# First half's mixes: who reads the transposes' bank, and who hands it back

## The reference

```
xn = layernorm(x)
xs = shift of xn by one token (zero first)
xm = xn * time_mix + xs * (1 - time_mix)          # the "mix"
k = exp(min(xm @ Wk.T, 60)); v = xm @ Wv.T; r = xm @ Wr.T
wkv, sum_k = decaying sums over earlier tokens of k*v and of k, per channel
attn = (sigmoid(r) * wkv / sum_k) @ Wo.T
z   = layernorm(xn) * ln_gamma + ln_beta
gamma = max |z| over the WHOLE input               # needs every token before any use
ffn = clip(z * 128 / gamma) @ ternary(weight) * (gamma * beta / 128)
out = x + attn + ffn
```

## Time and profile before

| what | value |
| --- | --- |
| median of three runs | 912.33 us |
| profiled execution | 912.93 us, span 911.1 us |
| TensorE busy | 878.0 us, 96% |
| VectorE busy | 761.6 us, 84% |
| ScalarE busy | 509.1 us, 56% |
| GpSimd busy | 188.5 us, 21% |
| share of TensorE in the chain that ended last | 71% (VectorE 17%, ScalarE 4%) |
| line 590 (removed operation) | 32 times, 21.7 us, mean 679 ns |
| line 861 (VectorE's mix before) | 32 times, 22.2 us, mean 696 ns |

### The profile page before, as it was taken

One profiled execution on the slowest core, in us unless ns is written; L12 is line 12 of the kernel. 1 busy time (PEld: TensorE's weight loads), 2 busy tenths in 40 slices (PEclk: granted clock), 3 DMA queues, 4 the chain that ended last, 5 costly groups with the idle time before them and its releaser, 6 DMA issues.

```text
span 911.1 us, 12736 instructions
## 1 busy us (share of the span) xinstructions
PE 878.0 (96%) x3984; PEld 713.5 (78%) x3984; DVE 761.6 (84%) x1282; ACT 509.1 (56%) x830; POOL 188.5 (21%) x242
## 2 busy tenths in 40 slices
PE   2989999999999999999999999999999999999998
PEld 2768777787878777787888888888888888888886
DVE  5998988889798988889897887878878878789684
ACT  3674756757575756747555464653635545455441
POOL 5442334134243323231010010100201002011000
PEclk9999999999999999999999999999999999999999
DMA  8221405142321405144543444243432543334311
GB/s 277 105 81 73 159 26 186 32 150 70 138 92 69 162 7 179 56 150 109 190 133 122 139 151 153 68 159 138 147 107 79 196 138 98 109 128 139 93 47 46
DMA packets 59841, 107.13 MB, mean 118 GB/s; under 512 B 7712, under 2 KB 7712, under 8 KB 59808
## 3 DMA queue, kind: packets, MB, share of 16 engines
q1 hardware_dynamic: 59808, 106.73, 34.8%
HBM read 64.76 MB, written 41.96 MB: 117 GB/s over the span
## 4 chain that ended last, share of the span: by engine, by line
PE 71%; DVE 17%; issue 5%; ACT 4%; DMA 1%; SPq 0%; DVEq 0%; ACTq 0%
PE kvr L492 13%; PE kvr L494 13%; PE kvr L493 13%; PE out_banks L528 6%; PE out_banks L530 6%; PE out_banks L507 6%; PE out_banks L510 6%; PE out_banks L509 6%; DVE scans L942 4%; DVE bn_stats L805 2%; PE transposed L450 2%; DVE rwkv_lo L962 1%; DVE k_and_kv L932 1%; DVE absmax L868 1%; DVE k_and_kv L958 1%
## 5 line engine op out<-in xcount | busy, mean ns | idle before, releaser
L1195 POOL TENSOR_TENSOR evacuated<-normed,mix_over_ffn_row 128x512 f32<-128x512 f32 x28 | 36.3, 1298 | 353.2 <-DVE ffn_lo L885 353.2
L492 PE MATMUL kvr<-xm_hi,wk_hi 128*128 128x512 f32 x256 | 103.8, 405 | 4.0 <-DVE xm_lo L885 4.0
L492 PE MATMUL kvr<-xm_hi,wv_hi 128*128 128x512 f32 x256 | 102.8, 402 | 1.4 <-DVE k_and_kv L932 0.9
L492 PE MATMUL kvr<-xm_hi,wr_hi 128*128 128x512 f32 x256 | 103.4, 404 | 0.0
L507 PE MATMUL out_banks<-wo_hi,rwkv_hi 128*128 128x512 f32 x256 | 101.9, 398 | 0.5 <-DVE rwkv_lo L962 0.5
L510 PE MATMUL out_banks<-wo_hi,rwkv_lo 128*128 128x512 f32 x256 | 101.2, 395 | 0.0
L509 PE MATMUL out_banks<-wo_lo,rwkv_hi 128*128 128x512 f32 x256 | 101.2, 395 | 0.0
L494 PE MATMUL kvr<-xm_hi,wk_lo 128*128 128x512 f32 x256 | 100.8, 394 | 0.0
L494 PE MATMUL kvr<-xm_hi,wr_lo 128*128 128x512 f32 x256 | 100.5, 393 | 0.0
L493 PE MATMUL kvr<-xm_lo,wk_hi 128*128 128x512 f32 x256 | 100.4, 392 | 0.0
L493 PE MATMUL kvr<-xm_lo,wr_hi 128*128 128x512 f32 x256 | 100.1, 391 | 0.0
(11 more groups left out here) (125 smaller groups left out, 1910.1 us busy)
## 6 DMA issues: line engine op xcount, KB each, us to landing
other<-ffn_input SPq DMA_DIRECT2D x64, 256.0 KB, 5.4
x<-in_x SPq DMA_DIRECT2D x15, 1024.0 KB, 5.8
other<-in_x SPq DMA_DIRECT2D x8, 1024.0 KB, 5.6
ffn_input<-evacuated SPq DMA_DIRECT2D x32, 256.0 KB, 4.6
ffn_input<-parked SPq DMA_DIRECT2D x32, 256.0 KB, 2.1
attn_scratch<-x SPq DMA_DIRECT2D x8, 1024.0 KB, 4.4
parked<-attn_scratch SPq DMA_DIRECT2D x8, 1024.0 KB, 7.2
out<-parked SPq DMA_DIRECT2D x8, 1024.0 KB, 5.2
```

What stands on the lines that cost most here:

```text
L492: nc.tensor.matmul(KVR[:, m, :], hi, XH[t][:, ch, :], start=(ch == 0), stop=False)
```

## The change

In the first half VectorE takes the token's own part from the transposes' bank and multiplies it by `time_mix` in the same operation that adds the shifted part. ScalarE makes the shifted part alone. As VectorE is now the last reader of the bank, TensorE's slots wait for `dve_x` besides `act_u`.

```diff
             def slot(b, ph, n):
                 kind, ch = slot_of(ph, n)
+
+                pe.wait_ge(dve_x, splits_before(b, ph, n))
                 pe.wait_ge(act_u, slots_before(b, ph, n))
...
                 elif mix:
-                    if ph != "P":
-                        nc.scalar.activation(U[:, r, :], bank, ACT.Copy, scale=tmx[:, ch:ch + 1])
                     nc.scalar.activation(WS[:, n % 2, :], bank, ACT.Copy,
                                          scale=tmx1[:, ch:ch + 1]).then_inc(act_u, 1)
...
                 dve.wait_ge(act_u, m + 1)
-                if ph == "P":
-
-                    bank, scale = first_banks[n], tmx[:, ch:ch + 1]
-                    V.tensor_copy(last_x[:, ch:ch + 1], WS[:, n % 2, TILE - 1:TILE])
-                    V.tensor_scalar(U[:, r, 0:1], bank[:, 0:1], scale, None, ALU.mult)
+                if kind.startswith("mix") and ph != "B":
+
+                    bank, scale = first_banks[n] if ph == "P" else TB[:, :], tmx[:, ch:ch + 1]
+                    if kind.endswith("0"):
+                        V.tensor_copy(last_x[:, ch:ch + 1], WS[:, n % 2, TILE - 1:TILE])
+                        V.tensor_scalar(U[:, r, 0:1], bank[:, 0:1], scale, None, ALU.mult)
+                    else:
+                        V.scalar_tensor_tensor(U[:, r, 0:1], bank[:, 0:1], scale, last_x[:, ch:ch + 1],
+                                               ALU.mult, ALU.add)
                     V.scalar_tensor_tensor(U[:, r, 1:TILE], bank[:, 1:TILE], scale, WS[:, n % 2, 0:TILE - 1],
                                            ALU.mult, ALU.add).then_inc(dve_x, 1)
...
-                elif kind.startswith("mix"):
-
-                    if kind.endswith("0"):
-                        V.tensor_copy(last_x[:, ch:ch + 1], WS[:, w, TILE - 1:TILE])
-                    else:
-                        V.tensor_tensor(U[:, r, 0:1], U[:, r, 0:1], last_x[:, ch:ch + 1], ALU.add)
-                    V.tensor_tensor(U[:, r, 1:TILE], U[:, r, 1:TILE], WS[:, w, 0:TILE - 1],
-                                    ALU.add).then_inc(dve_x, 1)
```

## The result

The changed kernel took 955.42 us (median of 4 runs, 953.61 to 957.15) against 912.45 us for the one before. The ratio is 1.0465, 95% interval 1.0452 to 1.0477: slower by 43 us. The forecast was 951.3, range 939 to 957.

What follows compares the result with a forecast made beforehand. TensorE, busy 96%, was taken to bound the kernel. Waits of 32.3 less 4.5 us given back, plus 11.2 us of lower clock, made 39.0 us on 912.93 profiled; 951.3 us as median, range 939 to 957.

Steps and rivals of the forecast that it cites:

- What bounds the kernel: Whole kernel: TensorE, busy 96% of the span; time is lost or won where it stands still.
- First hand-over: Slots 8 to 9 and 20 to 21, eight groups: TensorE waits for VectorE's late mix, 32.3 us in all.
- Second and third hand-over: Slots 9 to 10 to 11 and 21 to 22 to 23: no further waits; 4.5 us given back at the third.
- the 4.5 us given back: Third hand-overs, slots 11 and 23: old waits vanish as ScalarE has one bank read and TensorE comes later.
- not slower: Rival: first slot's mix done before TensorE wants the bank; 908 us; chance 0.05 together with "no change".
- TensorE's clock: Behind the long first hand-over pauses: granted clock falls at seven of eight, 1.6 us each, 11.2 us in all.
- the one case before: Batch 0, before the transposes at 54.40: a 2.69 us pause, then a clock fall taken to cost 1.6 us.
- upper bound of 19 us: Clock term's upper limit: all eight pauses bring the fall, with a stretch half as long again at the lower level.
- The sum: Whole kernel: 27.8 us of net waits plus 11.2 us of clock, 39.0 us on the profiled 912.93.
- the mechanism that came true: First half: TensorE's standstill plus the fall of its clock, range 947 to 955 us, chance 0.70.
- every hand-over waits: Rival: third and sometimes second hand-overs fail by 0.5 us; 955 us, up to 959; chance 0.12.
- The second half: Second half of the kernel: no instruction changes, so it should last the same.

Runs made afterwards that it cites:

- the wait alone: The kernel before, with only TensorE's slots also waiting for VectorE's `dve_x`; ScalarE still makes both parts: 957.77 us, ratio 1.049.
- one mix moved: The changed kernel, with VectorE's mix of slots 8 and 20 moved ahead of the two scans of the recurrence: 920.50 us, ratio 1.0086.
- the relief of ScalarE without the long pauses: The changed kernel without the second semaphore; in the first half VectorE multiplies its SBUF buffer's contents instead of reading the bank: 911.13 us, ratio 0.9978.
- the busy pauses: The changed kernel, with 12 extra matmuls of unused result before the waiting transposes of slots 9 and 21: 939.14 us, ratio 1.0289.
- two mixes early: The changed kernel, with VectorE's mixes of slots 8 and 20 before the recurrence's scans and of 9 and 21 behind them: 915.21 us, ratio 1.0025.
- the same order with the old mix: The kernel before, with mixes of slots 8, 9, 10, 20, 21, 22 early and ScalarE reading 10 and 22 before the logarithm: 912.30 us, ratio 0.9994.

## Why the prediction was right, and the term that was too small

- *What bounds the kernel.* TensorE, and its pauses: right. The loss lies in the distances between its transposes, at the first and second hand-overs.
- *First hand-over.* 32.3 us forecast, 32.6 measured, eight waits of 2.3 to 4.5 us. The lag could be read from the trace before because VectorE's backlog there waits for nobody. The run with the wait alone brings the pauses back with the old mix, and the run with one mix moved takes them away. VectorE's pair takes 175.90 - 175.03 = 0.87 us in `mix_own1`, 0.88 forecast; from PSUM the wide operation takes 0.74 us, as the rows before had it. The 62 more cycles of the Trainium skill (VectorE: DVE Perf Modes, the section on the TRN2 errata) show in none of these rows.
- *Second and third hand-over.* No further waits: right, and the 4.5 us given back came as 4.4. But the relief of ScalarE without the long pauses gives only 1.9 us. In that run the third hand-overs got 2.7 us shorter and not 4.5: those of `mix_next0` still took 3.6 to 3.7 us instead of 3.2. And 1.6 us came back as waits at the output product. In the changed kernel, where TensorE's pauses let VectorE catch up, all of them took 3.2. The rival "not slower" named 908 us for a kernel without long pauses; the run that comes nearest to it took 911.1. Its gain of 4.5 us was too high by 2.6.
- *TensorE's clock.* The mechanism was right, the term "7 x 1.6 = 11.2 us" mis-sized: it measured 17.1 us in the trace, and 16.3 us by the busy pauses. Two things were off. All eight pauses brought the fall, that of 2.29 us too, which the prediction had left out for being shorter than the one in the trace before (2.69). And the one case before was at the cheap end: the eight cost 1.46 to 2.85 us, 2.1 on average, since the lower level lasted from about 3 to 6 us. The upper bound of 19 us given for this term held. That one case was also weaker ground than it looked: the same pause, 2.69 to 2.74 us in all ten profiles, brought no fall in two of them (two mixes early, and the same order with the old mix). The seven pauses of 3.7 us and more all brought it, here and in the run with the wait alone.
- *The sum.* It has 39.0 us of loss, the profile 43.2. The clock is 5.9 us more than forecast, and the first and third hand-overs are 0.4 more (32.6 - 4.4 against 27.8). The distances elsewhere, which the sum put at nothing, are 2.1 us less. So two errors in part cancelled, and the total came nearer than its largest term. The result also lies just past the 947 to 955 us given to the mechanism that came true, where "every hand-over waits" was priced; that rival did not happen, as the second hand-overs waited for nobody and the third ones took 3.2 us.
- *The second half.* Unchanged: right, 474.3 against 474.1 us.

## What to carry to other kernels

When a buffer of which there is only one gets a new last reader, look up in the trace when that reader comes to the operation, not how long it takes: here 0.87 us of work handed the bank back 4 us late, because it stood behind a backlog that had cost nothing so far. Each of the eight pauses of the matmul engine, 2.3 to 4.5 us long, cost another 1.5 to 2.9 us of slow matmuls behind it, so count a long pause with more than its own length. Where the new reader must stay, move its operation in its queue and follow what the move delays, on both engines: the first move here brought back 35 us, the next ones ran into the logarithm behind the recurrence and then into the last low part.

## What the runs showed of the hardware

- All 14 pauses of TensorE of 3.67 to 4.46 us (changed kernel and the wait alone) were followed by a stretch at 1.2 GHz. Of the 12 of 2.19 to 2.74 us in the ten profiles, 10 were, and two, of 2.71 and 2.70 us, were not. The two shortest of these, 2.19 and 2.29 us, came only 7 us behind another pause, so they may not stand for their length alone. Behind pauses of 1.10 to 1.80 us in front of slots 9, 10, 21 and 22 the next slot came in 3.2 to 3.3 us, with no sign of a fall.
- The length of one pause doesn't settle it. In the start of the kernel before, the level fell with shorter pauses, where TensorE did only three matmuls between them, 18.16 and 20.42 us into the profile:

```profile
18.16 0.47 PE L492 MATMUL kvr<-xm_hi,wk_hi 128*128 128x512 f32 x1 [1.71 <-DVE xm_lo L885]
20.42 0.79 PE L492 MATMUL kvr<-xm_hi,wk_hi 128*128 128x512 f32 x1 [1.33 <-DVE xm_lo L885]
...
20.00:22.00 2.00, 1.58 (x3) 0.83 (x3) 1.18 (x4) 1.21 (x2) 1.57 (x3) 0.54 0.31 117
```

- The cost of one fall varied from 1.46 to 2.85 us with nearly equal pauses (3.84 us: 2.72; 3.91 us: 1.56), and four runs of the changed kernel spread over 3.5 us, against 0.2 us for four with the pauses kept busy.
- Extra matmuls whose result is overwritten made a kernel faster by 16 us, since they kept the clock up.
